# Product keys, top keys and routed experts: instruction order, bank slots and batch overlap on one core

## The reference

```python
# product keys: two sets of 32 keys per head, 8 heads, 1024 experts, top 8 of 64 pairs
q = (xn @ w_q.T).reshape(b, t, 8, 2, 128)
s1, i1 = top_k(sim(q[..., 0, :], keys_0), 8); s2, i2 = top_k(sim(q[..., 1, :], keys_1), 8)
fs, pk = top_k(s1[..., :, None] + s2[..., None, :], 8)      # over the 64 pairs
hidden = gelu(xn . expert_down[picked]) * relu(fs)
out = sum(hidden * expert_up[picked])

# top keys ("gathered values"): 4096 keys, the best 8 values are fetched per token
h_final = scan(h @ A + x @ Bm);  h_proj = h_final @ W_imp.T
importance = softmax over s of (x . h_proj);  token_pref = softmax over n of (x @ W_router.T)
neuron_w = einsum('bs,bsn->bn', importance, token_pref);  neuron_w /= neuron_w.sum(-1) + 1e-8
Q = x @ einsum('bn,ndr->bdr', neuron_w, compress)           # compress: 64 x 128 x 128
scores = Q @ K.T / sqrt(128);  topk_scores, topk_idx = top_k(scores, 8)
out = einsum('bskd,bsk->bsd', V[topk_idx], softmax(topk_scores))

# routed experts: 8 experts, top 2, hidden width 176, bf16 products with f32 sums, f32 shared expert
scores = sigmoid(x @ gate_w.T);  sel = top_k(scores + expert_bias, 2)
routed = sum over sel of (relu((x * score) @ w_up.T) ** 2) @ w_down.T
out = routed + (relu(x @ shared_w_up.T) ** 2) @ shared_w_down.T
```

## Time and profile before

| | |
|---|---|
| median of the three runs | 2315.13 us (2308.87 to 2318.24) |
| time of the profiled execution | 2313.05 us |
| its span in the trace | 2311.2 us |
| instructions | 33205 |
| busy share of the span | PE 84%, PEld 57%, DVE 69%, ACT 52%, POOL 27% |
| granted TensorE clock, mean | 0.90 |

### The profile page before, as it was taken

One profiled execution on the slowest core, in us unless ns is written; L12 is line 12 of the kernel. 1 busy time (PEld: TensorE's weight loads), 2 busy tenths in 40 slices (PEclk: granted clock), 3 DMA queues, 4 the chain that ended last, 5 costly groups with the idle time before them and its releaser, 6 DMA issues. The chain is left out here.

```text
span 2311.2 us, 33205 instructions
## 1 busy us (share of the span) xinstructions
PE 1950.1 (84%) x10882; PEld 1310.8 (57%) x10882; DVE 1595.5 (69%) x3840; ACT 1203.7 (52%) x2540; POOL 630.5 (27%) x774
## 2 busy tenths in 40 slices
PE   8999789996799995799999999987778776775897
PEld 5666544443577773587778777774324333334544
DVE  4555457785278887388898899873368666676676
ACT  3333355652355542588788877850245444554343
POOL 2222147776012122000000000000055555554111
PEclk9999989997899997799999999996688888887877
DMA  2000010000200000000000000005011111111100
GB/s 83 27 27 18 33 66 1 19 10 10 91 10 10 19 10 5 24 1 6 15 6 3 14 6 6 6 1 198 1 36 38 44 48 47 48 45 56 51 27 27
DMA packets 35266, 68.90 MB, mean 30 GB/s; under 512 B 8598, under 2 KB 19935, under 8 KB 34359
## 3 DMA queue, kind: packets, MB, share of 16 engines
q1 hardware_dynamic: 26934, 50.34, 6.3%
q0 software_dynamic: 8192, 16.79, 2.8%
HBM read 54.52 MB, written 12.58 MB: 29 GB/s over the span
## 5 line engine op out<-in xcount | busy, mean ns | idle before, releaser
L2758 PE MATMUL tk_to_act<-tk_keys,tk_xT 128*128 128x512 f32 x512 | 270.3, 672 | 94.9 <-issue 57.9
L1996 ACT ACTIVATE pk_sums<-pk_sum 128x512 f32<-128x512 f32 x512 | 278.8, 601 | 110.2 <-PE pk_sum L2216 107.8
L2088 DVE SCALAR_TENSOR_TENSOR pk_level<-pk_sums,pk_least 128x1024 f32<-128x1024 f32 x256 | 321.5, 1276 | 7.7 <-ACT pk_sums L1996 6.4
L2442 POOL DMA_INDIRECT tk_values<-top_keys_values,tk_index x256 | 243.9, 953 | 299.0 <-DVE tk_index L2607 224.3
L2224 PE MATMUL pk_weights<-product_keys_early_ident,pk_level 128*128 128x128 f32 x2048 | 271.8, 276 | 31.2 <-DVE pk_level L2088 30.1
L2224 PEld LDWEIGHTS pk_weights<-product_keys_early_ident,pk_level 128*128 128x128 f32 x2048 | 225.5, 141 | 65.1 <-DVE pk_level L2088 49.5
L2507 ACT ACTIVATE tk_scores<-tk_to_act 128x512 f32<-128x512 f32 x256 | 143.3, 594 | 209.7 <-PE tk_to_act L2758 112.3
L2758 PEld LDWEIGHTS tk_to_act<-tk_keys,tk_xT 128*128 128x128 f32 x512 | 101.5, 212 | 243.5 <-issue 181.9
L1667 PEld LDWEIGHTS er_outs<-experts_early_w,er_hT 128*128 128x128 f32 x1024 | 134.0, 192 | 59.8 <-issue 56.4
L1102 PE MATMUL ml_outs<-experts_early_we,ml_xT 128*128 128x512 f32 x320 | 162.5, 635 | 3.0 <-DVE ml_r L967 3.0
L2605 DVE MAX8 tk_best<-tk_scores 128x8 f32<-128x4096 f32 x32 | 141.4, 4418 | 32.1 <-issue 16.3
(11 more groups left out here) (396 smaller groups left out, 3731.5 us busy)
## 6 DMA issues: line engine op xcount, KB each, us to landing
tk_scores<-top_keys_compress SPq DMA_DIRECT2D x1, 4096.0 KB
tk_values<-top_keys_values,tk_index POOLq DMA_INDIRECT x256
att_x_proj<-x_first SPq DMA_DIRECT2D x4, 512.0 KB, 5.2
att_x_res<-x_first SPq DMA_DIRECT2D x4, 512.0 KB
x_after_attention<-att_y SPq DMA_DIRECT2D x4, 512.0 KB
ml_x<-x_after_attention SPq DMA_DIRECT2D x4, 512.0 KB, 3.4
experts_early_w<-experts_w SPq DMA_DIRECT2D x2, 1024.0 KB
x_after_attention<-ml_y SPq DMA_DIRECT2D x8, 256.0 KB, 2.0
```

The source lines that it names most:

```text
L1996: act.activation(sums[:, n % SUMS, half * HALF:(half + 1) * HALF], bank[:], ACT.Copy).then_inc(S.free.sem, 1)
L2088: dve.scalar_tensor_tensor(level[:, n % LEVELS, :], sums[:, n % SUMS, :], least[:, t % 2, h:h + 1], sums[:, n % SUMS, :], ALU.is_ge, ALU.m ...
L2442: pool.indirect_dma_start(out=values[:, slot, k, :], out_offset=None, in_=c["values"], in_offset=bass.IndirectOffsetOnAxis(ap=index[slot][ ...
L2758: pe.matmul(bank[:], xT[:, b, at * P:(at + 1) * P], keys[:, ch * HALF:(ch + 1) * HALF], start=True, stop=True).then_inc(S.full.sem, 1)
```

## The change

Three stages are edited.

Product keys: `keep(t, h)` now stands ahead of `weigh(t - 1)`, and TensorE's first `build_sum` of a tile ahead of its wait for `weighed_ready`:

```diff
+                    keep(t, h)
                     if h == 0 and t > 0:
                         weigh(t - 1)
-                    keep(t, h)
                     if t + 2 < ALL:
                         if h == 1:
...
+                    build_sum(next_built(t * HEADS + h))
+                    if h == 0:
                         after(pe, weighed_ready, t)
-                    build_sum(next_built(t * HEADS + h))
                     if chained:
                         if h >= HEADS - FILLS:
```

```diff
+            def prefer(b):
+                for g in range(HALVES):
+                    if L.must_wait(0):
+                        pe.wait_ge(L.free.sem, L.to_claim(0))
+                    bank = L.claim()
+                    for i in range(PER_HALF):
+                        t = g * PER_HALF + i
+                        ins = pe.matmul(bank[:, i * NEURONS:(i + 1) * NEURONS], xT[:, b, t * P:(t + 1) * P], router[:, 0:NEURONS],
+                                        start=True, stop=True)
+                    ins.then_inc(L.full.sem, 1)
...
+                for t in range(TILES):
+                    ins = pe.matmul(importance[:, b, t:t + 1], xT[:, b, t * P:(t + 1) * P], router[:, NEURONS + b:NEURONS + b + 1],
+                                    start=True, stop=True)
+            ins.then_inc(importance_full, 1)
...
-            for n in range(NEURONS):
-                ins = pe.transpose(to_act[0][:, n * 2 * B:(n + 1) * 2 * B], squeeze_rows[:, n, :], ident[0:2 * B, 0:2 * B])
+            for n in range(HALF_RANK):
+                ins = pe.matmul(to_act[0][:, n * 2 * B:(n + 1) * 2 * B], compress[:, n, :], neuron_pair[:], start=True, stop=True)
             ins.then_inc(squeeze_full, 1)
```

```diff
-                    pe.matmul(bank[:], xT[:, b, at * P:(at + 1) * P], keys[:, ch * HALF:(ch + 1) * HALF],
-                              start=True, stop=True).then_inc(S.full.sem, 1)
+                    for half in range(2):
+                        first = ch * WIDE + half * HALF
+                        ins = pe.matmul(bank[:, half * HALF:(half + 1) * HALF], xT[:, b, at * P:(at + 1) * P],
+                                        keys[:, first:first + HALF], start=True, stop=True)
+                    ins.then_inc(S.full.sem, 1)
                 if t >= MIX_LAG:
...
+            def root(g):
+
+                group = half_of(g)
                 pool.wait_ge(moments_ready, (g + 1) * PER_HALF)
-                rsqrt_on_pool(steps, pool, rstd[:, half_of(g)], moments[:, half_of(g), 1], plus_eps[:], eps[:], power[:]).then_inc(rstd_ready, 1)
+                after(pool, offset_ready, g)
+                steps.do(pool.tensor_tensor(minus_mean[:], moments[:, group, 0], minus_one[:], ALU.mult))
+                steps.link(rsqrt_on_pool(steps, pool, rstd[:, group], moments[:, group, 1], plus_eps[:], eps[:], power[:]))
+                pool.tensor_tensor(offset[:, group], minus_mean[:], rstd[:, group], ALU.mult).then_inc(offset_ready, 1)
...
                 act.wait_ge(best_ready, t + 1)
+                act.activation(minus[:, slot, :], best[:, slot, 0:1], ACT.Copy, scale=-1.0).then_inc(minus_ready, 1)
...
+            def normalise(t):
+                g, at = divmod(t, PER_HALF)
+                own = t % KEPT_R
+                if at == 0:
+                    act.wait_ge(offset_ready, g + 1)
+                    after(act, stored[g % HALVES], 16 * (g // HALVES))
+                act.activation(y[:, t % TILES, :], r[:, own, :], ACT.Identity, bias=offset[:, own:own + 1],
+                               scale=rstd[:, own:own + 1]).then_inc(y_ready, 1)
...
+                    act.activation(scores[:, t % KEPT, ch * WIDE:(ch + 1) * WIDE], bank[:], ACT.Copy).then_inc(S.free.sem, 1)
                 if t >= 1:
...
                 after(dve, mixed, t + 1 - SLOTS)
-                steps.link(dve.max(best[:, slot, :], scores[:, t % KEPT, :]))
-                dve.tensor_scalar(minus[:, slot, :], best[:, slot, 0:1], -1.0, None, ALU.mult).then_inc(best_ready, 1)
+                dve.max(best[:, slot, :], scores[:, t % KEPT, :]).then_inc(best_ready, 1)
+                dve.wait_ge(best_ready, t + 1)
```

```diff
+            def take_out(b, g):
+                half = b * HALVES + g
+                act.wait_ge(out_full, half + 1)
+                after(act, turned_full, half - 1)
+                act.activation(outT[:, g, :], outs[g][:], ACT.Copy).then_inc(outT_ready, 1)
...
+            def project_down(unit):
+                g, pair = divmod(unit % UNITS, PAIRS)
+                for k in range(PER_UNIT):
+                    n = unit * PER_UNIT + k
+                    units, w = (P, down[:, 2 * pair + k, :]) if k < 2 else (2 * TAIL, down_tail[:, pair, :])
+                    pe.wait_ge(hidden_ready, n + 1)
+                    ins = pe.matmul(outs[g][:], w, hidden[0:units, n % HIDDEN_SLOTS, :], start=False,
+                                    stop=pair == PAIRS - 1 and k == PER_UNIT - 1)
+                if pair == PAIRS - 1:
+                    ins.then_inc(out_full, 1)
+
+            def turn_out(b, g):
+                half = b * HALVES + g
+                pe.wait_ge(outT_ready, half + 1)
+                after(pe, turned_free, half)
+                for i in range(PER_HALF):
+                    ins = pe.transpose(turned[:, i * P:(i + 1) * P], outT[:, g, i * P:(i + 1) * P], ident[:])
+                ins.then_inc(turned_full, 1)
...
+            for unit in range(ALL):
+                b, u = divmod(unit, UNITS)
+                more = b + 1 < B
+                if unit + 1 < ALL:
+                    widen(unit + 1)
+                project_up(unit, range(2))
+                if unit >= DOWN_LAG:
+                    project_down(unit - DOWN_LAG)
+                project_up(unit, range(2, PER_UNIT))
+                if more and u in (0, 1):
+                    transpose_x(b + 1, u)
+                if u == 2 and b > 0:
+                    turn_out(b - 1, 1)
+                if more and u == 2:
+                    gates(b + 1)
+                if u == 3:
+                    shared_project(b, 1)
+                if more and u in (4, 5):
+                    for i in range(2):
+                        shared_hidden(b + 1, 2 * (u - 4) + i)
+                if more and u == 5:
+                    transpose_parts(b + 1)
+                if u == 6:
+                    turn_out(b, 0)
+                if more and u == 7:
+                    shared_project(b + 1, 0)
+            for unit in range(ALL - DOWN_LAG, ALL):
+                project_down(unit)
+            turn_out(B - 1, 1)
```

670 lines of the change are left out of this document (337 added, 333 removed).

## The result

The changed kernel takes 2282.74 us (median of four runs, 2280.59 to 2289.95), beside 2312.72 for the kernel before in the same comparison: a ratio of 0.987, 95% interval 0.984 to 0.991, 30 us faster. I had forecast 2214 and a range of 2152 to 2268. The profiled execution took 2289.95 us with a span of 2287.8, the slowest of the four.

What follows compares the result with a forecast made beforehand. No engine was full in the three stages; serial chains, waits and late TensorE signals during GpSimd's gathers bound them. Terms -21 -8 -45 +1 -28 = -101 gave 2214 us, range 2152 to 2268.

Steps and rivals of the forecast that it cites:

- the term of -45: Scores loop: fewer TensorE signals, nine to five per tile, shorten stalls by 59 us, less 14 for GpSimd's slower pace.
- rival 1: Scores loop: the delay isn't per signal and stays, so the loop gives 0, not -45: 2259 us; chance 0.20.
- Rival 3: Scores loop: only GpSimd running out of indices ends stalls; at one in two tiles +97, 2356 us; chance 0.05.
- Rival 2: Scores loop: stalls vanish because GpSimd's root pauses are longer; the loop gives -92, 2167 us; chance 0.13.
- -8: Preamble of top keys: sum of router move, shorter chain, new squeeze and dropped `twice`, -8 us, bounds -20 and +12.
- the -3.5: Preamble: saving in the router pass after the fold, left with only the importance column, 3.5 us.
- The chain's saving of 8.2: Preamble: wide VectorE passes, big exponential with its table load and the sum go beside other work, -8.2 us.
- the early router's cost of 9: Preamble: the router's 32 matmuls, moved beside the loads, add 7 to 14 us early; +9 taken.
- -21: Product keys: reordering on VectorE and TensorE saves 0.67 us per tile, -21 us, bounds -10 and -38.
- -28: Routed experts: overlapping batches make VectorE's work the pace, -28 us, bounds -10 and -42.
- the fear of half clock: Routed experts: 8 to 10 us allowed for stretches at half clock, in which a unit is TensorE's.
- Rival 4: Routed experts: TensorE stays at half clock and overlapping gives -10, 2232 us; chance 0.62 shared with the forecast.

Runs made afterwards that it cites:

- e3: The changed kernel with the score banks as before, four of 512 and eight score signals per tile: 2288.5 us beside 2314.2 for the kernel before (0.988).
- e9: The changed kernel, GpSimd waiting before every second tile until the gathers of the tile before have landed: 2209.5 us on chip 3, ratio 1.0034 to the kernel before.
- e10: The changed kernel, GpSimd waiting behind each tile's first gather until the gathers of the tile before have landed: 2189.8 us on chip 3 (0.993).
- e8: The changed kernel with only VectorE's half of the product-keys swap, TensorE's first build_sum back behind its wait for weighed: 2289.2 us beside 2311.4.
- e15: The changed kernel with GpSimd waiting for the mix of tile t - 5, the narrow weighted sum and the old squeeze: 2215.0 us beside 2311.1 (0.958).
- e17: The changed kernel with narrow weighted sum, old squeeze and GpSimd waiting before every eight gathers for the landing of the tile before: 2219.3 us beside 2311.1 (0.961).
- e7: The changed kernel with the squeeze as before the change, 16 matmuls with 512 columns moving, 16 copies and 64 transposes: 2275.2 us beside 2311.4.
- e16: The changed kernel with narrow weighted sum, old squeeze and GpSimd waiting for the mix and the next scores' copies: 2217.3 us beside 2311.1 (0.960).
- e6: The changed kernel with the preferences held once, so the weighted sum has 64 stationary columns per matmul and not 128: 2277.9 us beside 2311.4.

## Why the prediction was wrong

**The scores loop** (the term of -45). The step that failed reads: "at 3.9 us a signal, a tile needs 35 us with nine and 19.5 with five; what exceeds 10.15 falls from 25 to 9.4, to 0.38". I had averaged four late arrivals over the length of one stall and called the mean a price. But the length was set by something else. A stall begins when VectorE needs a mix whose signal waits; GpSimd then works off the indices that it has, up to one tile of 10 us, and 2 to 4.3 us after its last gather VectorE has its mix. Five signals per tile give stalls of 12 to 17 us and nine give 14 to 16 (one of 7), which is what e3 shows, and the idle time before the reciprocal was 125.4 us where I had said near 45. The row that told it stood in my own text: VectorE at 1857.65 and ScalarE at 1857.69, released together. I gave that to rival 1 with a chance of 0.20, and rival 1 is what happened, loop 0. The 14 us that I booked for GpSimd's longer root don't show either; that its slack in the stalls hides them is my reading, and no run tests it. Rival 3's mechanism is right (a stall is ended only by GpSimd running out) and its frequency wrong: one stall in four tiles, before and after. Rival 2, no stalls, is what e9 and e10 show on chip 3, for a reason that I had not thought of.

**The preamble** (-8, measured +11.3, at the edge of my bounds of -20 and +12). Three terms. The squeeze, which I put at 15.5 us since "that stretch ran at 0.90", ran at 0.50 and took 27.45, my own upper figure. The 0.90 belonged to the old form with its 512 moving columns, and that too began at half clock (1.86 us for the first pair, 1.02 from the fourth on); I carried the mean clock of one stream over to another that moves 8. The second term I left out: doubling `pref` doubles the stationary columns of 64 instructions, 6.98 us to 13.79. The row was there (128x64 operands at half the time of the 128x128 ones). The third is the -3.5 for the router pass after the fold: it took 13.78 us where it had taken 13.73, because, as my own text says, both versions load the same weights 64 times. The chain's saving of 8.2 measured 8.6, and the early router's cost of 9 measured 6.6.

**Product keys** (-21, measured -16.7). Right in sign and near in size, but in part by luck, since the reason is wrong: I counted TensorE's two waits, 0.57 us a tile, and e8 shows that its swap gives nothing. What counts is VectorE's order. Its level filled its own wait until ScalarE's copies became late: the four kinds of wait shown above, 54.0 us together before, fell to 40.0, which is 14 of the 16.7 us.

**Routed experts** (-28, measured -29.4). The size is as forecast. VectorE is busy 95.6 of 105 us in the middle, as I had it, but TensorE, which I called the lesser, 101.9 at a clock of 0.97; the fear of half clock was not borne out. Both sides vary, though: the second profile of the kernel before has the stage at 164.4, and the same code of the changed one takes from 139.4 (e10) to 147.2 us (e3). From all of them the change is -17 to -32, and the hit within 1 us is partly luck.

Rival 4 had no part in it. The range failed by 15 us: its upper end lay 9 us above rival 1 (2259), and with rival 1 came the preamble's 19 us and 4 of product keys.

## What to carry to other kernels

When waits end all at once, look for the one event that ends them before pricing them one by one: a mean over a stall says nothing of what each signal costs. Where an engine that issues indirect transfers back to back shares a pipeline with TensorE, give it a short pause of its own, or a wait for the signal that the others want (e15 and e17 are worth the same); it can pay more than taking signals away. Time it on more than one chip: on chip 3 e9, with its pauses, is 0.3% slower than the kernel before, and e10 0.7% faster; the changed kernel alone was not run there. And before exchanging a few long matmuls for many short ones, price the weight loads at half clock and count the stationary columns.

## What the runs showed of the hardware

- While GpSimd issues indirect transfers without a pause (0.30 us between them), what TensorE has finished is seen by ScalarE and VectorE up to 21 us late (a mix that ended at 2046.59 was seen at 2067.49; with a pause, 0.04 us late), and ScalarE's signals to TensorE are prompt in the same stretch (0.06 us). The same bytes as direct transfers by SyncE delay nothing (loop 347.6 us).
- A pause of GpSimd of 2.27 us after eight gathers is enough to let them through, one of 0.61 us isn't (loops of 426.0 and 464.3 us).
- This differs by chip: on one of the four that are numbered here (one session on it) the same program, with the same short pauses, has no such stalls (382.5 for 464.3 us), and the kernel before takes 2202 us there for 2311 to 2316 on the other three. Why is open.
- Granted clock beside what ran: TensorE stayed at 0.50 (1.2 GHz) through 128 instructions with 8 moving columns (27.45 us). In e7, with 32 of 512 columns, it began at that level too (1.87 us for the first pair) and was at 1.02 us for a pair from the fifth on; in e16 from the third on.
- The time of a one-column matmul went with its stationary columns: 64 instructions took 6.99 us with 64 of them (e6) and 13.79 with 128, both at 0.50.
